# Mask add and row maximum fused on DVE, small DVE steps as tensor-tensor, cross scores by row halves, in a three-stage decoder kernel

## The reference, cut to what matters

```python
# cross-attention, 8 heads of 16 features
scores = jnp.einsum('bthd,bshd->bhts', q, k) / np.sqrt(HEAD_DIM)
scores = jnp.where(src_mask[:, None, None, :] == 0, -jnp.inf, scores)
attn = jax.nn.softmax(scores, axis=-1)
...
# windowed attention, 6 layers, 16 heads of 64 features, window 32
q = l2norm(q) * qs          # l2norm(t) = t / max(norm(t), 1e-12)
k = l2norm(k) * ksc
q = q * cos * scale + rotate_half(q) * sin * scale
k = k * cos * inv + rotate_half(k) * sin * inv
mask = (it < jb) | (it > jb + w) | (jb == -1)
sim = jnp.einsum('bhwie,bhwje->bhwij', bq, bk2) * QK_SCALE
sim = jnp.where(mask, -jnp.finfo(sim.dtype).max, sim)
attn = jax.nn.softmax(sim, -1)
out = jnp.einsum('bhwij,bhwje->bhwie', attn, bv2)
```

## Time and profile before

| | us |
|---|---|
| median of three runs | 4879.15 |
| lowest and highest | 4876.62, 4883.68 |
| the profiled execution, its time | 4873.85 |
| its span, first to last instruction | 4872.0 |
| stages one and two | about 795 |
| one layer of stage three | about 676 |
| turns of attention, steady | about 4.5 each |

### The profile page before, as it was taken

The page is one execution under the profiler, slowest core; times in us unless marked ns, Lnnn a source line. Parts: engine busy times, 40 slices in busy tenths (PEclk is TensorE's granted clock), DMA queues, the critical chain, the costliest instruction groups (busy, mean ns, idle before and its releaser), DMA issues.

```text
span 4872.0 us, 114175 instructions
## 1 busy us (share of the span) xinstructions
PE 4404.6 (90%) x33552; PEld 3380.6 (69%) x33552; DVE 3955.4 (81%) x8237; ACT 3046.9 (63%) x11581; POOL 2973.6 (61%) x3009
## 2 busy tenths in 40 slices
PE   7888887999998999989999989999899999899998
PEld 5676765777766777657777667777577776677775
DVE  5666666888878888778888788888788887888885
ACT  2444444777746777647777467777377775577773
POOL 2333334777746777647777467777377774577771
PEclk9999997999999999999999999999999999999999
DMA  4222220000000000000000000000000000000000
GB/s 138 75 84 70 80 74 18 0 0 0 0 19 6 0 0 0 0 24 1 0 0 0 19 6 0 0 0 0 24 1 0 0 0 18 6 0 0 0 0 18
DMA packets 75916, 82.96 MB, mean 17 GB/s; under 512 B 13622, under 2 KB 69396, under 8 KB 74836
## 3 DMA queue, kind: packets, MB, share of 16 engines
q1 hardware_dynamic: 75732, 80.87, 5.1%
HBM read 45.34 MB, written 35.52 MB: 17 GB/s over the span
## 4 chain that ended last, share of the span: by engine, by line
PE 53%; DVE 24%; issue 15%; ACT 5%; DVEq 1%; POOL 1%; DMA 0%; SPq 0%; ACTq 0%; POOLq 0%; PEldq 0%
PE bank_pair L1001 8%; PE bank L983 7%; PE bank L1016 7%; DVE pTl L1136 6%; PE bank L456 5%; PE bank L458 3%; PE bank L457 3%; DVE own_crossed L1092 3%; PE bank_pair L998 3%; PE bank L1008 3%; DVE own_crossed L1094 3%; DVE ss L1104 3%; PE bank L600 2%; ACT sc L625 2%; PE bank_pair L1211 2%
## 5 line engine op out<-in xcount | busy, mean ns | idle before, releaser
L1067 ACT ACTIVATE p<-bank_pair,mx 128x128 f32<-128x128 f32 x3072 | 1088.4, 366 | 654.4 <-DVE mx L1120 654.4
L1170 POOL TENSOR_TENSOR p<-p,ri 128x512 f32<-128x512 f32 x768 | 799.7, 1041 | 341.9 <-DVE ri L1112 341.9
L1166 POOL TENSOR_TENSOR rot<-own_crossed 128x512 f32<-128x512 f32 x768 | 983.3, 1280 | 29.4 <-DVE own_crossed L1094 29.4
L1120 DVE TENSOR_REDUCE mx<-bank_pair 128x4 f32<-128x512 f32 x768 | 528.7, 688 | 380.5 <-PE bank_pair L1001 369.8
L1160 POOL TENSOR_TENSOR rot<-rot,rn 128x512 f32<-128x512 f32 x768 | 804.2, 1047 | 32.4 <-DVE rn L1125 11.1
L983 PE MATMUL bank<-pTl,v_sb 128*64 128x128 f32 x6144 | 509.0, 287 | 217.8 <-DVE pTl L1136 217.3
L456 PE MATMUL bank<-wqkv_hi,xs_lo 128*128 128x512 f32 (+1 forms) x1536 | 668.4, 435 | 38.4 <-DVE own_crossed L1094 21.4
L1067 ACT ACTIVATION_READ_ACCUMULATOR p<-bank_pair,mx 128x1 f32 x3072 | 624.0, 203 | 0.0
L1045 ACT ACTIVATE qkT<-bank 128x512 f32<-128x512 f32 x768 | 456.4, 594 | 234.0 <-PE bank L974 234.0
L983 PEld LDWEIGHTS bank<-pTl,v_sb 128*64 128x64 f32 x6144 | 322.6, 137 | 375.5 <-DVE pTl L1136 235.7
L1001 PE MATMUL bank_pair<-qkT 64*128 64x128 f32 x6144 | 550.1, 298 | 0.0
(11 more groups left out here) (199 smaller groups left out, 8629.8 us busy)
## 6 DMA issues: line engine op xcount, KB each, us to landing
pos_scratch<-pos_sb SPq DMA_DIRECT2D x32, 1020.0 KB, 4.3
sc<-pos_scratch SPq DMA_DIRECT2D x32, 512.0 KB, 4.0
own_crossed<-in_L_ffn_Wqkv SPq DMA_DIRECT2D x6, 1536.0 KB, 6.7
ctx_sb<-in_ctx SPq DMA_DIRECT2D x32, 128.0 KB, 3.5
wo<-in_L_ffn_Wo SPq DMA_DIRECT2D x6, 512.0 KB, 7.1
mrow<-in_mask_BxS_fk SPq DMA_DIRECT2D x1, 2048.0 KB, 7.7
x_all<-in_x SPq DMA_DIRECT2D x4, 512.0 KB, 8.7
out<-res SPq DMA_DIRECT2D x8, 256.0 KB, 2.2
```

The costliest lines, as they stand in the source:

```text
L1067: last = nc.scalar.activation(p[:, j, h, :], s_ps[:, h % 2, h // 2 * T:(h // 2 + 1) * T], ACT.Exp, bias=mx[:, j, h % 2, h // 2:h // 2 + 1] ...
L1166: nc.gpsimd.tensor_tensor(rot[:, j4, :, :], own[:, j4, :, :], crossed[:, j4, :, :], ALU.add).then_inc(L["rot0"], 1)
L1170: nc.gpsimd.tensor_tensor(p[:, j, :, :], p[:, j, :, :], ri[:, j, :].unsqueeze(2).to_broadcast([128, G, T]), ALU.mult).then_inc(L["pn"], 1)
```

## The change

- **Mask and maximum.** The two bf16 mask matmuls go. The four score products no longer accumulate on them. DVE replaces its reduction by four fused operations of 128 columns, one per head: each adds `band_f` from SBUF to a head's scores in PSUM, writes the negated sum to `p` in SBUF and the minimum of it, the negated row maximum, to `mx`. Each is two instructions, the operation and one that writes out its accumulator. PE's next scores wait for `mx` and no longer for `exp`.
- **Exp.** ACT computes exp in place from `p` in SBUF, with scale -1, and no longer from PSUM. Its wait on T2 (the transposition of the unit four before) moves to DVE.
- **Small steps.** `ssc`, `root_err` and `rn` become tensor-tensor operations. The constants that a scalar operand carried move into a table of ones and a half, a table of the clamp's floor, the scale of ACT's Square and Ln, and the rotary tables. `root_err` becomes two operations: a product in place in `root_sq`, and a subtraction.
- **Cross scores.** `kexp` has four heads' copies instead of eight: rows 0 to 63 hold heads 0 to 3, rows 64 to 127 heads 4 to 7. Each of PE's two matmuls takes 64 rows.

```diff
-    return (np.arange(D)[:, None] // DX == np.arange(HX)[None, :]).astype(np.float32)
+    return (np.arange(D)[:, None] // DX % (HX // 2) == np.arange(HX // 2)[None, :]).astype(np.float32)
...
-                        last = nc.tensor.matmul(W1b[j][:, :], q2T[:, :], kexp[:, HALF * j:HALF * (j + 1), :].rearrange("p h n -> p (h n)"), start=True, stop=True)
+                        rows = slice(HALF * DX * j, HALF * DX * (j + 1))
+                        last = nc.tensor.matmul(W1b[j][:, :], q2T[rows, :], kexp[rows, :, :].rearrange("p h n -> p (h n)"), start=True, stop=True)
...
-                    nc.gpsimd.tensor_tensor(kexp[:, :, :], kT[:, :].unsqueeze(1).to_broadcast([128, HX, T]),
-                                            heads[:, :].unsqueeze(2).to_broadcast([128, HX, T]), ALU.mult).then_inc(S1["kexp"], 1)
+                    nc.gpsimd.tensor_tensor(kexp[:, :, :], kT[:, :].unsqueeze(1).to_broadcast([128, HALF, T]),
+                                            heads[:, :].unsqueeze(2).to_broadcast([128, HALF, T]), ALU.mult).then_inc(S1["kexp"], 1)
...
-                        pe.wait_ge(L["exp"], n(6))
-                    for odd in range(2):
-                        nc.tensor.matmul(s_ps[:, odd, :], ident_bf[:, :], band_bf[:, :, :].rearrange("p h n -> p (h n)"), start=True, stop=False, skip_group_check=True)
+                        pe.wait_ge(L["mx"], n(6))
                     for h in range(G):
                         r = slice(h % 2 * DL, h % 2 * DL + DL)
-                        last = nc.tensor.matmul(s_ps[:, h % 2, h // 2 * T:(h // 2 + 1) * T], qkT[r, j, h // 2, :], qkT[r, j, 2 + h // 2, :], start=False, stop=(h // 2 == 1), skip_group_check=True)
+                        last = nc.tensor.matmul(s_ps[:, h % 2, h // 2 * T:(h // 2 + 1) * T], qkT[r, j, h // 2, :], qkT[r, j, 2 + h // 2, :], start=True, stop=True)
...
-                    if reused(first, k, 6, 4):
-                        act.wait_ge(L["T2"], n(6) - 3)
                     for h in range(G):
-                        last = nc.scalar.activation(p[:, j, h, :], s_ps[:, h % 2, h // 2 * T:(h // 2 + 1) * T], ACT.Exp,
-                                                    bias=mx[:, j, h % 2, h // 2:h // 2 + 1], scale=1.0, accum_out=psums[:, j, h:h + 1])
+                        last = nc.scalar.activation(p[:, j, h, :], p[:, j, h, :], ACT.Exp, bias=mx[:, j, h:h + 1], scale=-1.0, accum_out=psums[:, j, h:h + 1])
...
-                    dve.wait_ge(L["root_sq"], m + 1)
-                    nc.vector.scalar_tensor_tensor(root_err[:, jm, :, :], root_sq[:, jm, :, :], -0.5 * ROOT_GAIN ** 2, ssc[:, jm, :, :], ALU.mult, ALU.mult).then_inc(L["root_err"], 1)
+                    dve.wait_ge(L["root_sq"], 2 * m + 1)
+                    nc.vector.tensor_tensor(root_sq[:, jm, :, :], root_sq[:, jm, :, :], ssc[:, jm, :, :], ALU.mult).then_inc(L["root_sq"], 1)
+                if newton:
+                    dve.wait_ge(L["root_sq"], 2 * m + 2)
+                    nc.vector.tensor_tensor(root_err[:, jm, :, :], onehalf[:, :, :], root_sq[:, jm, :, :], ALU.subtract).then_inc(L["root_err"], 1)
                 if on(6):
-                    dve.wait_ge(L["S"], n(6) + 1)
                     if reused(first, k, 6, 4):
-                        dve.wait_ge(L["exp"], n(6) - 3)
-                    nc.vector.tensor_reduce(mx[:, (k - 6) % 4, :, :], s_ps.rearrange("p o (h n) -> p o h n", h=2), X_AXIS, ALU.max, negate=True).then_inc(L["mx"], 1)
+                        dve.wait_ge(L["T2"], n(6) - 3)
+                    wait_apart(dve, L["S"], n(6) + 1)
+                    for h in range(G):
+                        last = nc.vector.tensor_tensor_reduce(p[:, (k - 6) % 4, h, :], s_ps[:, h % 2, h // 2 * T:(h // 2 + 1) * T], band_f[:, :], -1.0, -3 * MASKED, ALU.add, ALU.min,
+                                                              mx[:, (k - 6) % 4, h:h + 1])
+                    last.then_inc(L["mx"], 1)
...
-                    nc.vector.scalar_tensor_tensor(rn[:, jr, :, :], root_err[:, jm, :, :], 1.5, root0[:, jm, :, :], ALU.add, ALU.mult).then_inc(L["rn"], 1)
+                    nc.vector.tensor_tensor(rn[:, jr, :, :], root_err[:, jm, :, :], root0[:, jm, :, :], ALU.mult).then_inc(L["rn"], 1)
...
-                    nc.vector.tensor_scalar(ssc[:, jm, :, :], ss[:, jm, :, :], 1e-24, None, ALU.max).then_inc(L["clamp"], 1)
+                    nc.vector.tensor_tensor(ssc[:, jm, :, :], ss[:, jm, :, :], ss_least[:, :, :], ALU.max).then_inc(L["clamp"], 1)
```

19 lines of the change are left out of this document (12 added, 7 removed).

## The result

The changed kernel takes 5252.64 us (median of four runs, 5248.86 to 5258.83) against 4878.08 us for the kernel before (four runs): a ratio of 1.0767, with a 95% interval of 1.0748 to 1.0785. That is 374 us slower, and 43 us beyond the upper end of the predicted range. Its profiled execution took 5249.47 us, with a span of 5247.7.

What follows compares the result with a forecast made beforehand. No engine was taken as the bound, but a dependency ring of 18.00 us per four turns. Terms of -41, +35 and +153 gave +147 on the profiled 4873.85, or 5021; with 5 for the median, 5026 us, range 4825 to 5210.

Steps and rivals of the forecast that it cites:

- the ring: Third stage: dependency loop through ACT, POOL, DVE and PE that closes once in four turns, taken as 18.00 us.
- rival 4: DVE's small steps in tensor-tensor form escape POOL and nothing is blocked: -0.84 us a ring, 4682 us; chance 0.05.
- the sum: The forecast's terms together: cross scores -41, mask, maximum and exp +35, blocked groups +153, in all +147 us.
- the tie: Turn 3: DVE's new product and POOL's L1160 start about together, so one group in two is blocked: +153 us.
- rival 2: Turn 3: the product always comes second to POOL, so every group is blocked: +307 us, 5180 us; chance 0.25.
- the block's price: A blocked product in turn 3 makes `pTl` of turn 0, and the ring with it, 1.65 us late.
- The caught clamp: Turn 0 of a blocked group: DVE's clamp, at +7.5 us, runs into POOL's next L1160 and ends at +8.4.
- the row maximum: DVE, turn 2: four heads of the fused operation take 1.10 us against 0.60, +0.50 us a ring; bounds 0.85 and 1.50.
- rival 3: The fused operation takes only 0.85 us for four heads and the product comes first: 4827 us; chance 0.10.
- Cross scores -41: PE's cross scores: two row halves run beside each other, saving half of four steps, -41 us in all.
- Masks -0.48 a ring: PE ahead of the scores: two mask matmuls of 0.12 us go, passed twice in a ring, -0.48 us.
- Exp from SBUF +0.17: ACT's exp of four heads, read from SBUF, takes 0.17 us longer on the ring; range 0.08 to 0.17.

Runs made afterwards that it cites:

- `xs_hi` late: The changed kernel with ACT's `xs_hi` moved behind `root0` in turn 3, so that POOL starts later: 4921.3 us.
- `xs_hi` early: ACT's `xs_hi` moved to the head of its turn 2: 4762.49 us on the changed kernel, 4726.88 us on the kernel before.
- the filler: The changed kernel with twelve dead PE matmuls in turn 0 ahead of the wait for `pTl`, and the `oT` wait moved ahead of them: 5083.77 us.
- 4883.81: The changed kernel with the kernel before's two operations for `root_err` and `rn` in place of the three: 4883.81 us, ratio 1.0013.

## Why the prediction was right or wrong, point by point

**Right: direction, place and mechanism.** Slower, all of it in the ring of the third stage, and by the step I named: a third dependent small step that is blocked and then blocks the next. The tensor-tensor form does not escape POOL (rival 4 is out). The two kinds of operation that the change brings in went apart in the trace: in 180 groups the steps with two SBUF inputs were blocked to the end of POOL's instruction (965 and 1194 ns on average), and the fused operation, with one SBUF input, ran at 285 ns on average and 294 at most. That the fused one is free of POOL no row of before showed, and the sum took it so; in the kernel after, 1706 of its 3072 executions began with over 0.35 us of a POOL operation to go, and these took 285 ns on average and 293 at most. A single SBUF input does not free a step by itself, though: the clamp in its old form has one and was held as well, 1198 times in the 14 traces. What decided for the small steps is what POOL had begun, as the rows of the run with `xs_hi` late show, with 0.17 and 0.97 us for the same form.

**Wrong: the tie.** The sum took one group in two as blocked; it was every steady group, rival 2's case. The step that failed is "at a tie with POOL": I had the product 0.20 behind `root_sq` and POOL 0.21 or 0.16. In the 180 steady groups of the kernel after, POOL's L1164 stands 0.14 behind (median), and the product 0.25, never less than 0.19. The sum had `root_sq` done 0.17 after its start, and that is the part that failed: with exp 0.17 later, `root_sq` begins while `xs_lo` is under way in all 180 groups, and in 158 of them it is held to 0.03 behind the end of `xs_lo` (in the rows above, 1708.12 + 0.20 = 1708.32, against 1708.28). The product follows 0.03 later, while POOL's L1164 has begun 0.04 ahead of the end of `xs_lo`. So the product stands 0.10 or 0.11 behind L1164 in 166 of the 180 groups, and further behind it in the rest: `root_sq` and L1164 both go by the end of `xs_lo`, and there was no tie to be had. In the run of the small steps alone, where `root_sq` has its 0.17, the product stood 0.17 or 0.21 behind POOL, and was blocked as often. Only an order that is turned round, as with `xs_hi` early, freed it.

**Wrong: no term for the clock.** PE's waits for `pTl` were in the sum as time alone. They grew to 2.2 us in turn 0, and behind most of them the granted clock fell to the lower level. This cost at least 169 us by the filler and some 185 by the rings, and it is why the time lies beyond rival 2's 5180 and beyond the range.

**Mis-sized: the block's price.** It was forecast as 1.65 us a ring, with the clamp of turn 0 caught as well. Measured, the third step makes the ring 0.94 us longer where the clock stays up (0.96 with the filler, 200 us between the kernels of 5083.77 and 4883.81), as the clamp is free in those rings, and 2.48 where the clock falls and the clamp is caught as well. The caught clamp was foreseen, but it came by way of the clock.

**Mis-sized: the row maximum.** 1.10 us for four heads was taken, 0.85 is what it takes: the heads start 0.21 apart, and the accumulator's read of 0.08 begins together with the next head's operation. That was the lower bound and rival 3's value. It did not help, as DVE's later start on the scores (0.15) and `wo`'s later start (0.16 or 0.40, by the kind of ring) were missing from the sum: for the fused part it gave +0.19 a ring, +35 us; measured were +0.31 and +40.

**Right: the other terms.** Cross scores -41 (38 measured alone, 33 in the start of the third stage). Masks -0.48 a ring (-0.46). Exp from SBUF +0.17 (exp to `xs_hi` takes 1.55 instead of 1.39 us: +0.16), as these rows show, ACT first:

```profile
1705.76 0.40 ACT L1066 ACTIVATE p<-p,mx 128x128 f32<-128x128 f32 x1 [1.16 <-DVE mx L1122]
...
1707.31 0.29 ACT L1027 ACTIVATE xs_hi<-zS 128x128 fp32r x1
```

```profile
1704.79 0.29 DVE L1122 CUSTOM_DVE_ANT_0 p<-bank_pair,band_f 128x128 f32<-128x128 f32 x1 [1.16 <-issue]
```

Rival 2, with every block counted, comes within 73 us of the measured time, but by two errors that partly cancel: the block at the full clock is smaller than I had it (0.94 a ring and not 1.65), and it has no clock. With the clock's 185 us added it would be 5365.

**What stays open.** Of the 369 us that the third step costs, the 168 steady rings give 158 to the blocks (0.94 each) and some 185 to the clock; the rest lies at the ends of the layers and is not split. Why the clock stays up behind some of the waits of over 2 us is not known. Why the fused mask costs 38 to 40 us although it takes 18 us in 300 off PE is shown in part only: the wait ahead of `wo` was found, and not taken away.

## What to carry to other kernels

Before adding a small step that reads SBUF to a chain on VectorE, look in the timeline at what GpSimd has begun at that moment, and check whether the step ahead of it is held too: each dependent step here paid to the end of the operation it met, so a third one paid 1.0 us although it takes 0.17, and moving one GpSimd trigger was worth more (155 us on the kernel before, 490 on the one after) than any change of the steps' form. When a change makes TensorE wait longer at one place of a loop, compare the granted clock before and after as well (here 0.977 and 0.926 over the span), and price the lower level as a term of its own (here some 185 us). A part measured alone can hide such a step: here the three parts summed to 204 us and together cost 374.
